# Row slots, a fourth decay buffer and GpSimd sums in a one-core tower of five small layers

## What is computed

```
h = token_part(ids)                       # embedding, 2 reversible layers: attention + ffn
h = h + mamba_part(layernorm(h))          # forward and backward state-space scan, out_proj, ln, ffn, ln
h = h + moe_part(layernorm(h))            # 8 experts, top 2 weights, all 8 computed
h = h + attention(layernorm(h))           # 8 heads, head by head sums
h = h + nibble_alu(layernorm(h))          # small mlps, one-hot digits

# the scan, for each direction, 256 channels, 16 states:
dA = exp(dt * A);  h = dA * h + (dt * u) * B_t;  y = sum_s h * C_t

# the experts:
for e in range(8):
    y = gelu(x @ w1[e] + b1[e]) @ w2[e] + b2[e]
    out = out + comb[:, e:e + 1] * y
```

## Time and profile before

| what | value |
|---|---|
| median of 3 runs | 3996.34 us (3980.95 to 3997.95) |
| profiled execution, own time | 3997.05 us |
| its span, first to last instruction | 3995.0 us |
| first scan starts, last scan ends | 162.7 us, 3793.6 us |
| busy: DVE, PE, ACT, POOL | 87%, 79%, 72%, 38% |
| granted TensorE clock, mean | 0.885 |

### The profile page before, as it was taken

The page is one execution under the profiler, slowest core; times in us unless marked ns, Lnnn a source line. Parts: engine busy times, 40 slices in busy tenths (PEclk is TensorE's granted clock), DMA queues, the critical chain, the costliest instruction groups (busy, mean ns, idle before and its releaser), DMA issues.

```text
span 3995.0 us, 31171 instructions
## 1 busy us (share of the span) xinstructions
PE 3152.8 (79%) x8712; PEld 1357.8 (34%) x8728; DVE 3466.6 (87%) x4622; ACT 2891.6 (72%) x3785; POOL 1531.3 (38%) x708
## 2 busy tenths in 40 slices
PE   5666778878787878888787887878788787877797
PEld 3233233333333324333332433333343333322232
DVE  1399999999899998989999899989999999999932
ACT  2546686878778787878778787887878788766432
POOL 0345444444434443443434344343434434343300
PEclk8756889989898999989899998989899798988897
DMA  1233343434434343433434344333434344334310
GB/s 62 54 107 84 104 109 102 126 88 114 114 102 123 91 126 88 120 108 104 120 83 128 87 120 107 111 117 95 127 91 120 97 111 122 88 120 120 101 48 11
DMA packets 200829, 404.56 MB, mean 101 GB/s; under 512 B 17744, under 2 KB 26064, under 8 KB 200400
## 3 DMA queue, kind: packets, MB, share of 16 engines
q1 hardware_dynamic: 198608, 398.38, 36.8%
q0 software_dynamic: 2048, 4.20, 0.6%
HBM read 387.58 MB, written 14.94 MB: 101 GB/s over the span
## 4 chain that ended last, share of the span: by engine, by line
PE 31%; ACT 29%; DVE 26%; issue 12%; DMA 1%; POOL 1%; DVEq 0%; SPq 0%; ACTq 0%; another core or an unknown queue 0%; POOLq 0%
DVE states L859 7%; ACT decay L642 6%; ACT L642 6%; PE bank_a L506 6%; PE bank_b L517 5%; DVE states L865 5%; ACT L638 4%; ACT tok L642 4%; ACT last L642 3%; ACT middle L642 3%; DVE y_sum L870 3%; PE bank_a L458 2%; PE bank_p L415 1%; PE bank_p L358 1%; PE bank_c L577 1%
## 5 line engine op out<-in xcount | busy, mean ns | idle before, releaser
L1134 POOL TENSOR_TENSOR dbu<-dtu,bc_rows 128x1024 f32<-128x1024 f32 x512 | 1240.3, 2425 | 1962.5 <-DMA bc_rows<-bc_scratch 976.7
L859 DVE TENSOR_TENSOR_SCAN states<-decay,dbu 128x512 f32<-128x512 f32 x1024 | 1370.2, 1382 | 31.1 <-ACT decay L642 25.1
L506 PE MATMUL bank_a<-middle,experts 128*128 128x512 f32 x1024 | 596.3, 666 | 245.5 <-ACT middle L642 240.3
L642 ACT ACTIVATE middle<-bank_a,columns 128x512 f32<-128x512 f32 x608 | 417.9, 687 | 413.2 <-PE bank_a L506 342.2
L642 ACT ACTIVATE decay<-dt,neg_a 128x508 f32<-128x508 f32 x1024 | 662.7, 707 | 16.1 <-DVE states L859 12.9
L517 PE MATMUL bank_b<-middle,experts 128*128 128x512 f32 x1024 | 573.0, 643 | 56.7 <-DVE middle L1041 56.4
L865 DVE TENSOR_TENSOR states<-states,bc_rows 128x512 f32<-128x512 f32 x960 | 611.3, 680 | 0.4
L870 DVE TENSOR_TENSOR y_sum<-y_sum,states 128x512 f32<-128x512 f32 x960 | 610.1, 675 | 0.5
L642 ACT ACT_TABLE_LOAD x446 | 572.2, 1283 | 39.4 <-PEq L281 16.8
L506 PEld LDWEIGHTS bank_a<-middle,experts 128*128 128x128 f32 x1024 | 183.2, 203 | 583.6 <-ACT middle L642 385.9
L642 ACT ACTIVATE last<-bank_c 128x512 f32<-128x512 f32 (+2 forms) x320 | 201.8, 633 | 238.7 <-PE bank_c L533 67.5
(11 more groups left out here) (206 smaller groups left out, 4148.0 us busy)
## 6 DMA issues: line engine op xcount, KB each, us to landing
bc_rows<-bc_scratch SPq DMA_DIRECT2D x512, 512.0 KB, 5.0
experts<-ew SPq DMA_DIRECT2D x128, 512.0 KB, 6.3
comb_rows<-comb_scratch SPq DMA_DIRECT2D x128, 256.0 KB, 5.2
h_scratch<-tok SPq DMA_DIRECT2D x16, 256.0 KB, 2.5
x_scratch<-xin SPq DMA_DIRECT2D x16, 256.0 KB
xr<-x_scratch SPq DMA_DIRECT2D x16, 256.0 KB, 6.5
h<-h_scratch SPq DMA_DIRECT2D x16, 256.0 KB, 6.6
out<-last SPq DMA_DIRECT2D x16, 256.0 KB, 5.3
```

The costliest lines, as they stand in the source:

```text
L506: tick(mm(A, EW[:, e % 2, 128 * c:128 * c + 128], s_xn, start=True, stop=True), "e_h")
L642: return nc.scalar.activation(out, in_, func, **more)
L859: tick(nc.vector.tensor_tensor_scan(hs[:, h, ::step], da[:, n % AHEAD, h, ::step], dbu[:, n % AHEAD, h, ::step], 0.0, ALU.mult, ALU.add), ...
L1134: tick(nc.gpsimd.tensor_tensor(dbu[:, n % AHEAD], dtu[:, k % 2], b, ALU.mult), "a_dbu")
```

## The change

B and C rows get tiles of their own with three slots each, loaded by DMAs of their own of 256 KB (1024 instead of 512). The B row of state n waits only for `a_dbu` of state n-3, the C row only for `a_hc` of state n-3; SP issues the B row two states ahead of the C row. `decay` has four buffers. The experts' weighted outputs go by turns into `x1` and `part`, and the sum with `h2` is made by POOL. The first layer norm of `middle` writes `x1` and waits for the sum that read it. The ORDER strings of all engines are new, with one long first piece and no repeated one.

```diff
-SLOTS, AHEAD = 4, 3
+SLOTS, AHEAD, DECAYS = 3, 3, 4
 ORDER = {
-    "passes": 10,
+    "passes": 0,
...
-    da = sb("decay", [128, AHEAD, HALVES, T])
-    rows = sb("bc_rows", [128, SLOTS, 2, T])
+    da = sb("decay", [128, DECAYS, HALVES, T])
+    b_rows, c_rows = (sb(x, [128, SLOTS, T]) for x in ("b_rows", "c_rows"))
...
-                    if n >= AHEAD:
-                        act.wait_ge(s["a_scan"], HALVES * (n - AHEAD + 1))
+                    if n >= DECAYS:
+                        act.wait_ge(s["a_scan"], HALVES * (n - DECAYS + 1))
...
             def middle(g):
                 q = 3 * g
-                yield from ln("c_", q, A, s_sq, x1)
+                yield
+                if g:
+                    dve.wait_ge(s["e_acc"], NE * g - 1)
+                dve.wait_ge(s["c_rs"], q + 1)
+                tick(tt(x1, A, s_sq, ALU.mult), "c_ln")
...
-                    if n:
-                        dve.wait_ge(s["e_acc"], n)
+                    if e > 1:
+                        dve.wait_ge(s["e_acc"], n - 1)
                     dve.wait_ge(s["e_y"], NF * (n + 1))
-                    tick(stt(part, B, col(f"eb2_{e}"), cb[:, e % 2], ALU.add, ALU.mult), "e_t")
-                    yield
-                    if e == 0 and g >= 2:
-                        dve.wait_ge(s["a_out"], g - 1)
-                    if e == 0:
-                        dve.wait_ge(s["c_h1"], g + 1)
-                    dve.wait_ge(s["e_t"], n + 1)
-                    tick(tt(h2[g % 2], h2[g % 2] if e else h1[:, :], part, ALU.add), "e_acc")
+                    tick(stt((x1, part)[e % 2], B, col(f"eb2_{e}"), cb[:, e % 2], ALU.add, ALU.mult), "e_t")
...
+            def middle(g):
+                for e in range(NE):
+                    n = NE * g + e
+                    yield
+                    if e == 0 and g >= 2:
+                        pool.wait_ge(s["a_out"], g - 1)
+                    if e == 0:
+                        pool.wait_ge(s["c_h1"], g + 1)
+                    else:
+                        pool.wait_ge(s["e_acc"], n)
+                    pool.wait_ge(s["e_t"], n + 1)
+                    tick(nc.gpsimd.tensor_tensor(h2[g % 2], h2[g % 2] if e else h1[:, :], (x1, part)[e % 2], ALU.add), "e_acc")
...
-            drive("POOL", A=each(scan), P=each(gather), D=each(both))
+            drive("POOL", A=each(scan), P=each(gather), C=each(middle), D=each(both))
...
+                for k in (2 * g, 2 * g + 1):
+                    b_d, c_d = (rows_d[k % 2].rearrange("(c s a) t -> c s a t", c=2, a=1)[i] for i in (0, 1))
+                    for st in range(DS + 2):
+                        n = DS * k + st
+                        if st < DS:
+                            yield
+                            if st == 0:
+                                sp.wait_ge(s["p_wr"], 16 * k + 16)
+                            if n >= SLOTS:
+                                sp.wait_ge(s["a_dbu"], n - SLOTS + 1)
+                            sp.dma_start(b_rows[:, n % SLOTS], b_d[st, 0:1].to_broadcast([128, T])).then_inc(s[f"a_b{n % SLOTS}"], 16)
+                        if st >= 2:
+                            n -= 2
+                            yield
+                            if n >= SLOTS:
+                                sp.wait_ge(s["a_hc"], HALVES * (n - SLOTS + 1))
+                            sp.dma_start(c_rows[:, n % SLOTS], c_d[st - 2, 0:1].to_broadcast([128, T])).then_inc(s[f"a_c{n % SLOTS}"], 16)
```

More of the change, by code:

```diff
@@ L687, in pre @@
                 act.wait_ge(s["p_dtp"], 2 * k + 2)
[L688 removed]
+                link(act, af(e_sp, CE[:, :, :], ACT.Abs), "p_ex")
                 link(act, af(e_sp, e_sp, ACT.Exp, scale=-1.0), "p_ex")
@@ L724, in token @@
                 r = tok[:, 7:9]
-                link(act, af(nrm, nrm, ACT.Exp, scale=0.5), "t_nrm")
+                link(act, af(nrm, nrm, ACT.Exp, scale=0.5), "t_lr")
                 link(act, af(r, nrm, ACT.Ln, bias=col("small")), "t_lr")
@@ L1174, in scan @@
             def scan(g):
-                for n in range(2 * DS * g, 2 * DS * g + 2 * DS):
-                    yield
-                    k, st = n // DS, n % DS
-                    if st == 0:
-                        sp.wait_ge(s["p_wr"], 16 * k + 16)
-                    if n >= SLOTS:
-                        sp.wait_ge(s["a_dbu"], n - SLOTS + 1)
-                        sp.wait_ge(s["a_hc"], HALVES * (n - SLOTS + 1))
-                    pair = rows_d[k % 2].rearrange("(a c s) t -> s a c t", a=1, c=2)[st]
-                    sp.dma_start(rows[:, n % SLOTS], pair.to_broadcast([128, 2, T])).then_inc(s[f"a_row{n % SLOTS}"], 16)
+                for k in (2 * g, 2 * g + 1):
[15 more added lines that the diff above has]
+                            sp.dma_start(c_rows[:, n % SLOTS], c_d[st - 2, 0:1].to_broadcast([128, T])).then_inc(s[f"a_c{n % SLOTS}"], 16)
             def pre(d, g):
```

175 lines of the change are left out of this document (120 added, 55 removed).

## The result

The changed kernel took 3974.78 us (median of 20 runs), the kernel before 3995.16 us on the same chip: a ratio of 0.9943, 95% interval 0.9930 to 0.9956. It is 0.57% faster, where 2.0% was forecast. The profiled execution spans 3964.6 us against 3995.0, 30.4 us less; it is one of the quicker ones of the changed kernel (8 us under its median), so the profile shows 30 us where the medians differ by 20.

A forecast was written before the change was run, and what follows sets the result against it. DVE, busy 93% between first and last scan, was taken as the bound. From 3995.0 us, -92.8 + 0.6 - 9 + 25 + 8 + 50 - 84.6 + 60 - 35 gave a 3917.2 us span, forecast 3918 us, 2.0% faster; range 3835 to 4015.

The forecast's parts named there:

- the sums' term: The sums leave DVE for POOL: 99.0 us in all, -92.8 us for the fifteen groups in the scan phase.
- start: Before the first scan: token group 1's second layer norm now stands ahead of it, +8 us, ends 0 and +14.
- tail: After the last scan: more PE work shares it with group 15's experts, +25 us, and POOL's last sum adds +0.6.
- those started by a landing ... should go: Scans stretched by POOL products started at a row's landing: 99 us go; -35 us net of new POOL work.
- the fourth rival: Each sum on POOL holds up DVE by the port lock: 128 x 1.28 = 164 us, total 4044, chance 0.05.
- the third: Change of groups becomes the bound: ACT late, DVE waits 16 us instead of 8.4, total 4032, chance 0.12.
- the scan-started collisions stay: Collisions with products started at a scan's end stay unchanged, as 437 of 512 following steps are safe in both orders.
- The change of groups: Between groups, DVE waits 8.4 us for ACT's decays instead of 5.05: +50 us over 15 changes.
- The waits that were to go: DVE's waits at L859, the old L1111 and L920 mostly go with four decay buffers and more room: -84.6 us.
- three "short waits": Backward `dt`, first L1111 and a token layer norm stand close behind their makers: 1.5, 1.5, 1.0 us a group, +60.
- The first (the landings were the cost, sums free): All 99 us of landing stretches go and sums find PSUM steps beside them: 3854 us, chance 0.13.
- The second (the gain turns into waits): The experts' chain through PE and gelu comes 5 us later a group, 75 us return: 3993, no change, chance 0.20.

The follow-up runs named there:

- slots-alone run: Kernel before with three slots each for B and C rows and loads of their own; sums on DVE, three decays, old order: 3995.6 us.
- The three moves: Changed kernel with DVE's order changed at three places in 11 or 12 of 16 groups, putting PSUM-operand steps behind the scans: 3947.9 us.
- both edits and the moves: Changed kernel with `pre`'s two steps made by DVE, three moves in DVE's order, and L929 and L934 ahead of `pre` in 11 places: 3947.1 us.
- the cut sums: Changed kernel with POOL's sums of experts 1 to 7 cut to 8 of 512 columns: 3940.9 us.

## Why the prediction was right or wrong

Its direction was right, its size was not: 20 us instead of 78. It also said what a wrong forecast would look like, and none of that came: the wait at the change of groups is about 8 us, POOL waits for `b_rows` 15 times where it waited for a landing 257 times, and L923's mean of 1.407 us stays under 1.42. But DVE's busy time, forecast near 3333 us in total, is 3436.8, and L923's mean was to be near 1.33: the miss is in DVE's instructions. By its own terms, all for the profiled executions:

| term | forecast | measured |
|---|---|---|
| DVE's work without stretches (sums, and steps moved to the tail) | -90 | -89.5 |
| stretches (12 in the sums' term, 35 net beside it) | -47 | +55 |
| DVE's idle time in the scan phase (+50, -84.6, +60) | +25 | -37 |
| start | +8 | +16.3 |
| tail | +25.6 | +25.1 |
| sum | -78 | -30 |

**The sums' work and the tail** came out as priced. The first line is busy time less stretches, 3386.7 - 260.3 against 3351.9 - 315.0; of the forecast -92.8 - 9, some 12 were stretches of the old L1048, which the prediction's mean of 786 ns held.

**The landings.** The step "those started by a landing ... should go" is right: 119 us of such stretches became 13. Two readings beside it are not. The stretched pair of the earlier trace rows did not end "when POOL did": it ended at 1659.81, and POOL's product at 1657.61; what agrees is that it lost 1.2 us where POOL had 1.40 to run. And what the shared port could cost at worst is the fourth rival, not the third.

**The step that failed** is "the scan-started collisions stay", by which such stretches were priced at no change. It rested on a count of what follows each pair of scans, 437 of 512 safe in both orders. (In the traces 410 of these next steps have at most one SBUF operand before and 429 after, so such a count foretells no loss either way.) But it looked at one step only, and that one begins before the product does: those behind it are hit. In the kernel before 29 hits cost 31 us, 1.06 each, nearly all of them a pair of scans that begins when the product is half done. In the changed kernel 47 hits cost 80 us. Scans are again 25 us of it; 46 us are 11 instances each of L1079 and L1153. L1079 stands third behind the scans, with 0.4 us of small steps between, the first of which has a PSUM operand and counts as safe; L1153 stands behind L972. Each waits for nearly the whole product. Before, L1079's forerunner was hit once in this way and L1153's twice. And a part is the landings' doing: in the slots-alone run, with the old order, such stretches rose from 31 to 59 us and those of `pre` from 62 to 81, because products that had started late now start at the scan's end and hit what stands there. The three moves, of which two concern L1079 and L1153, took 42 us of stretch away and 27 from the time, which confirms the places.

**What the prediction left out** is POOL's queue. It priced each sum by itself (38 us; 47 measured, and 34 us of time when seven eighths were cut), and said that products queued behind a sum cost nothing, because they had time in hand. They were in time, but not in place: a product that starts late starts beside a pair of scans. The gathers, which the new order puts behind the third product of a group (before, behind the sixteenth), and the steps of `pre` brought 39 + 32 us in this way. The forecast named such queues only as a cause of waits, and priced them at 0.

**Idle time** was better than forecast by 62 us. The change of groups is right in size and in cause: 11.9 us from `dt` to the first scan, forecast 12.4, with ACT's decays last. That 8.4 us of waits lie in it is the same figure, though most of them stand before L1111. The waits that were to go went, but the forecast took them from the whole span: in the scan phase they were 63 us, not 84.6 (the scans for decays 25.1, the old L1111 20.0, L920 17.9), and now the last two have 2.5 and 0.5, and most of the scans' 21.8 lie at the change of groups. The three "short waits" of the new order, 60 us without a row, are small: in the steady groups the first L1111, the token layer norm and `pre` wait some 1 us together, not 4. And waits that the forecast left alone went as well: in the scan phase the router's L1012 13.9 us to nothing, the layer norms of `middle` (L834, now L1056 and L900) 18.9 to 8.6, L953 (now L1017) 8.1 to 0.3, L886 (now L950) 16.2 to 8.0. Against that stand the 38 us more of group 2, which no term names. So that the total idle time came out lower is in part luck of terms that cancel.

**The start** cost 16.3 instead of 8: the layer norm was ready at 177.8, 4 us earlier than in the earlier trace rows, and the scan began at 179.0 behind it.

**The rivals.** The first (the landings were the cost, sums free) is out: the slots alone gave nothing. The second (the gain turns into waits) is not what happened in the changed kernel, whose idle time fell, but it is exactly what happened in the slots-alone run, and it is what stops further gains: of the 81 us of busy time that both edits and the moves took away, 61 came back as waits. The third did not occur. The fourth, 1.28 us for each sum, is refuted by the cut sums (0.30).

**What stays open.** Which waits make up the limits of 228.7 and 223.5 us wasn't separated. That the new order owes its gain to the lower limit and not to a single step is shown only as a whole. With three decay buffers the new order wasn't tried. Why group 2 takes 259 us in the new order, and whether its strings could spare those 31 us, is open too.

## What to carry to other kernels

When a wait is removed, list the places where the released instruction will now start, and look at what runs there on the engine that it collides with: late starts may have been hiding bad places (28 us of them here). Look not only at the step directly behind the release but at all that begin while the released instruction runs: a safe step of 0.17 us covers nothing of a product of 2.36. Put the steps with a PSUM operand there until it is over, and small steps of two SBUF operands behind them; a 0.2 us step there costs as much as a large one. Before counting a gain on the busiest engine, cut sharply what lengthens its work in one run: here that showed, for the middle groups, a second limit 3.7 us (1.6%) under the period of the changed kernel, and, in the old order, one only 1.5 us under that of the kernel before, which no run in that order passed. And compare the groups one by one: the ends of a pipeline can gain what start and tail pay back.

## What the runs showed of the hardware

A DVE instruction with two SBUF operands that begins while POOL makes a product waits for the rest of the product, however small it is: L1079 with 32 columns took 2.20 us instead of 0.19, beside a product of 2.35. The Trainium skill (SBUF — State Buffer, section Who interferes with whom) says that such an instruction contends with a GpSimd instruction that reads SBUF; the row agrees. In the rows the loss doesn't depend on the DVE instruction's size.

When POOL had two products queued, the scan got no turn between them: one scan of 1.2 us took 5.78 us, close to its own 1.2 and the 4.65 of the pair.

In the other direction POOL is held up too: products of 2.36 us took up to 3.37. Beside L972, a 128x1024 step of two SBUF operands that had begun 0.2 us earlier, they took 3.25, and L1153 behind it then waited for that longer product.
